# Keys and values of a cross-attention layer by Strassen's seven products, one level, sums kept in PSUM

## What is computed

```python
h_q = (rmsnorm(layernorm(x)) @ w_q.T).reshape(b, lq, H, DH)
h_k = (key_value_states @ w_k.T).reshape(b, lk, H, DH)
h_v = (key_value_states @ w_v.T).reshape(b, lk, H, DH)
score = jnp.einsum('bqhd,bkhd->bhqk', h_q, h_k) + position_bias[None]
score = softmax(where(m, score, -inf)); score = where(m, score, 0)
attn = jnp.einsum('bhqk,bkhd->bqhd', score, h_v).reshape(b, lq, H * DH)
x = x + layernorm(x) + attn @ w_out.T
W = NF4_CODE[w_codes] * absmax                      # decoded weights
x = x + layernorm(x) @ W.T + 2 * (layernorm(x) @ W_a @ W_b)
```

## Time and profile before

| | |
|---|---|
| median of 3 runs | 870.4 us (869.73 to 871.6) |
| profiled execution | 869.9 us, its span 868.1 us, mean granted clock of TensorE 0.998 |
| PE busy | 857.5 us (99%), 4292 matmuls |
| DVE, ACT, POOL busy | 513.0, 340.3, 366.2 us |
| DMA | 60.79 MB, mean 70 GB/s |

### The profile page before, as it was taken

The page is one execution under the profiler, slowest core; times in us unless marked ns, Lnnn a source line. Parts: engine busy times, 40 slices in busy tenths (PEclk is TensorE's granted clock), DMA queues, the critical chain, the costliest instruction groups (busy, mean ns, idle before and its releaser), DMA issues.

```text
span 868.1 us, 13682 instructions
## 1 busy us (share of the span) xinstructions
PE 857.5 (99%) x4292; PEld 723.9 (83%) x4292; DVE 513.0 (59%) x781; ACT 340.3 (39%) x939; POOL 366.2 (42%) x341
## 2 busy tenths in 40 slices
PE   9999999999999999999999999999999999999898
PEld 6887888888888888888888888888888888888786
DVE  5658682387615775176823867157751778328683
ACT  5346261253414444153622535135341436225332
POOL 0996272162704345043630627034450436408730
PEclk9999999999999999999999999999999999999999
DMA  8112331032310323013220323103230132202002
GB/s 314 52 42 83 105 102 52 0 107 71 102 34 23 112 68 107 4 50 114 80 71 0 104 74 97 39 19 112 59 112 12 47 104 61 78 0 65 25 13 86
DMA packets 52581, 60.79 MB, mean 70 GB/s; under 512 B 11312, under 2 KB 33456, under 8 KB 52432
## 3 DMA queue, kind: packets, MB, share of 16 engines
q1 hardware_dynamic: 52560, 60.54, 23.5%
HBM read 42.14 MB, written 2.10 MB: 51 GB/s over the span
## 4 chain that ended last, share of the span: by engine, by line
PE 82%; POOL 9%; DVE 3%; SPq 2%; issue 2%; DMA 1%; ACT 1%; POOLq 0%; DVEq 0%
PE proj_ps L815 49%; PE out_ps L815 21%; PE out_ps L922 6%; PE s_ps L862 5%; POOL scratch L379 2%; POOL scratch L402 2%; SPq L271 2%; POOL scratch L405 1%; POOL resid L382 1%; POOL bias L371 1%; DMA v<-ctx_dram 1%; DVE qk_lo L614 1%; DVE p L671 0%; DMA pT<-p_turned 0%; PE proj_ps L875 0%
## 5 line engine op out<-in xcount | busy, mean ns | idle before, releaser
L371 POOL TENSOR_TENSOR bias<-pos_raw,mask_add 128x1024 f32<-128x1024 f32 x32 | 69.0, 2155 | 396.5 <-DVE p L671 395.7
L709 DVE TENSOR_TENSOR resid<-out_ps,resid 128x512 f32<-128x512 f32 x136 | 92.2, 688 | 238.6 <-PE out_ps L815 238.6
L402 POOL TENSOR_SCALAR scratch<-codes 128x256 f32<-128x256 int32 x120 | 157.2, 1310 | 19.8 <-POOL scratch L405 16.3
L505 ACT ACTIVATE p_blocks<-p,neg_max 128x128 f32<-128x128 f32 x248 | 96.1, 389 | 136.0 <-DVE neg_max L673 136.0
L442 ACT ACTIVATE v<-proj_ps 128x512 f32<-128x512 f32 x64 | 38.3, 598 | 196.8 <-PE proj_ps L815 196.8
L614 DVE TENSOR_TENSOR qk_lo<-qk_raw,qk_hi 128x512 fp32r<-128x512 f32 x64 | 100.8, 1576 | 7.6 <-ACT qk_hi L442 7.6
L815 PE MATMUL proj_ps<-ctx_hi,qk_hi 128*128 128x512 f32 x256 | 103.2, 403 | 0.3 <-DVE ctx_lo L614 0.3
L815 PE MATMUL proj_ps<-xn_hi,qk_hi 128*128 128x512 f32 x256 | 102.5, 400 | 0.1
L815 PE MATMUL proj_ps<-wv_hi,ctx_hi 128*128 128x512 f32 x256 | 100.6, 393 | 0.0
L815 PE MATMUL proj_ps<-wv_lo,ctx_hi 128*128 128x512 f32 x256 | 100.2, 392 | 0.0
L815 PE MATMUL proj_ps<-ctx_hi,qk_lo 128*128 128x512 f32 x256 | 100.2, 391 | 0.0
(11 more groups left out here) (111 smaller groups left out, 1445.1 us busy)
## 6 DMA issues: line engine op xcount, KB each, us to landing
pT<-p_turned SPq DMA_DIRECT2D x496, 32.0 KB, 1.8
qk_raw<-k_dram SPq DMA_DIRECT2D x32, 256.0 KB, 2.8
qk_raw<-q_dram SPq DMA_DIRECT2D x32, 256.0 KB, 2.7
wo_raw<-wo_dram SPq DMA_DIRECT2D x32, 256.0 KB, 2.8
wv_raw<-wv_dram SPq DMA_DIRECT2D x30, 256.0 KB, 3.5
resid<-x_dram SPq DMA_DIRECT2D x2, 1024.0 KB, 10.7
pos_raw<-pos_dram SPq DMA_DIRECT2D x32, 64.0 KB, 2.9
out_dram<-resid SPq DMA_DIRECT2D x8, 256.0 KB, 2.1
```

The lines of the kernel that those rows point to most:

```text
L371: pool.tensor_tensor(bias[:, :, :], pos, mask_add[:, :, :], ALU.add).then_inc(bias_done, 1)
L402: then(pool.tensor_scalar(level if code == 0 else picked, codes[:, :], float(code), value, match, ALU.mult))
L505: e = act.activation(out(b), p[:, b, :].rearrange("p (k c) -> p k c", c=Q), ACT.Exp, bias=neg_max[:, b:b + 1], accum_out=prob_sum[:, b:b + 1])
L709: dve.tensor_tensor(resid[:, b, :], out_ps[bank][:, :], resid[:, b, :], ALU.add).then_inc(out_drained, 1)
```

## The change

Keys and values, `ctx @ w`, are each cut once in halves of the tokens, of the inputs and of the heads, and the eight block products are replaced by Strassen's seven. The halves of heads are the two heads of a pair for the keys, and two pairs of a group for the values. Weight and context are kept as sums and differences of blocks:

- The seven sums of the context are made once at the start (POOL `context_sum`, then hi and lo) and fill `ctx_hi` and `ctx_lo`, [P, 7, 2, 512].
- The sums of weights are made in place in `k_raw` and `wv_raw` on POOL (`weight_sum`): four subtractions of 128x256 for each of 16 pairs of heads, four of 128x512 for each of 8 groups. Each waits until DVE has split the block that it overwrites.
- `key_product`: 6 matmuls of 512 columns, seven times a pair, all in the odd head of the pair. `value_product`: 12 matmuls of 256 columns, 14 times a group.
- The products are added up in PSUM banks; ACT copies a bank where a result or a partial sum is wanted (four copies), DVE adds a bank to what was copied (three additions), for keys for each pair, for values in two halves of tokens (r) for each group.
- There is one `k_raw` of a whole pair (512 KB), and its load for the next pair waits for the last split of the pair before it. On SP it is issued at odd heads behind both `move_blocks`; before, one head's 256 KB was issued ahead of them.
- To make room, the buffers `bias`, `p_turned` and `w_ffn` are gone: the bias is written into `p`, so `make_bias` waits for `exp_done` in place of `biased`; blocks are turned in place, so the first `exps` of a head waits for `pT_loaded` of the head before; decoded slices go to DRAM and come back, the last through `last_ffn_loaded`. Eight PSUM banks are shared out anew, and `attend` writes the two banks of the scores, after `biased`.
- The residual's hidden part moves from POOL to ACT, and `x_stage` from DVE to ACT.

```diff
+PRODUCTS = 7
+BLOCK_A, BLOCK_B, BLOCK_C, BLOCK_D = range(4)
+WEIGHT_AT = (BLOCK_A, BLOCK_A, BLOCK_A, BLOCK_B, BLOCK_D, BLOCK_C, BLOCK_A)
+BANK_OF = (0, 1, 0, 0, 1, 2, 0)
+OPENS = (True, True, False, False, False, True, False)
+SUMS = 4
+SUMS_FOR = (0, 1, 3, 2, 0, 0, 4)
+RING = 4
+COPIES = 4
+ADDS = 3
...
-                        sp.wait_ge(k_lo_done, h + 2)
-                        load_k(h + 2)
+                    if not final:
+                        sp.wait_ge(p_turned_done, 2 * h + 1)
+                        sp.sem_inc(sp_passed, 1)
+                        sp.wait_ge(attn_done, 2 * h)
+                        move_blocks((0, 1))
+                        sp.wait_ge(p_turned_done, 2 * h + 2)
+                        move_blocks((2, 3))
+                    if j % 2 and not last:
+                        sp.wait_ge(k_lo_done, PRODUCTS * (m + 1))
+                        load_k(m + 1)
...
+            def weight_sum(n, raw, sums, count, step):
+                out, plus, minus = ((BLOCK_A, BLOCK_B, BLOCK_A), (BLOCK_B, BLOCK_D, BLOCK_B),
+                                    (BLOCK_A, BLOCK_D, BLOCK_A), (BLOCK_A, BLOCK_C, BLOCK_A))[n]
+                if n:
+                    passed(sums, SUMS * count + n)
+                if n != 1:
+                    passed(step, PRODUCTS * count + (1, 0, 2, 3)[n])
+                pool.tensor_tensor(raw[:, out, :], raw[:, plus, :], raw[:, minus, :],
+                                   ALU.subtract).then_inc(sums, 1)
...
+            def make_bias(slot):
+                pos = pos_raw[:, slot, :].rearrange("p (o k) -> p o k", o=1).broadcast_to([P, B, L])
+                pool.tensor_tensor(p[:, :, :], pos, mask_add[:, :, :], ALU.add).then_inc(bias_done, 1)
...
+                    if j == 1:
+                        key_sum(2, m)
+                        key_sum(3, m)
+                    if j == 2 and not last:
+                        for n in range(SUMS - 1):
+                            key_sum(n, m + 1)
+                    if j == G:
+                        value_sum(2, g + 1)
+                    if not (last and j == G - 1):
-                        passed(biased, 2 * h + 2)
+                        passed(exp_done, 2 * h + 2)
+                        passed(pos_loaded[(j + 1) % 2], 16 * (2 * g + (j + 1) // 2 + 1))
+                        make_bias((j + 1) % 2)
+                    if j == 2 and not last:
+                        key_sum(SUMS - 1, m + 1)
+                    for quarter in (((0, 1), (2, 3), ())[j - 1] if last else (j - 1,)):
+                        decode(g, quarter)
+                    if j == 3 and not last:
+                        passed(wv_loaded, 16 * (g + 2))
+                        value_sum(0, g + 1)
+                        value_sum(1, g + 1)
+                    if j == G:
+                        value_sum(3, g + 1)
+                        key_sum(0, m + 1)
...
+            def odd_head(g, j, last):
+                h = G * g + j
+                m = 2 * g + (j + 1) // 2
+                exps(h, 0, by_blocks)
+                if j == 1:
+                    split_k(m, 2, key_slot(j, 2))
+                copy_keys(m, 0)
+                if j == 1:
+                    split_k(m, 3, key_slot(j, 3))
+                copy_keys(m, 1)
+                exps(h, 1, by_blocks)
+                for hf in range(2):
+                    attention(h - 1, j - 1, hf, s_flat(hf))
+                for p_at in (4, 5):
+                    split_k(m, p_at, key_slot(j, p_at))
+                copy_keys(m, 2)
+                split_k(m, 6, key_slot(j, 6))
+                drain_q(h + 1, 0, query_bank(j, 0))
+                for i in range(2):
+                    split_wo(i, 2 * g + j // 2 + 1, wo_hi)
+                drain_q(h + 1, 1, query_bank(j, 1))
+                split_q(h + 2)
+                if j == 3:
+                    split_v(g + 1, 0)
+                copy_keys(m, 3)
...
+            def even_head(g, j, last):
+                h = G * g + j
+                m = 2 * g + (j + 1) // 2 + 1
+                if j == G:
+                    split_v(g + 1, 1)
+                elif not last:
+                    split_k(m, 0, key_slot(3, 0))
+                for hf in range(2):
+                    exps(h, hf, by_blocks)
+                if j == 2 and not last:
+                    split_k(m, 1, key_slot(3, 1))
+                drain_q(h + 1, 0, query_bank(j, 0))
+                for hf in range(2):
+                    attention(h - 1, j - 1, hf, s_flat(hf))
+                if j == 2 and not last:
+                    split_k(m, 2, key_slot(3, 2))
+                    split_k(m, 3, key_slot(3, 3))
+                drain_q(h + 1, 1, query_bank(j, 1))
+                if not last:
+                    split_q(h + 2)
...
+            for hf in range(2):
+                exps(H - 1, hf, in_place)
+            act.wait_ge(last_ffn_loaded, 16)
+            split_ffn(C - 1)
+            for hf in range(2):
+                act.wait_ge(turned, hf + 1)
+                copy(last_pT[:, hf * HB:(hf + 1) * HB, :], s_ps[hf][:, :, :]).then_inc(last_pT_done, 1)
...
+            def add_keys(m, n):
+                slot, hf, bank, p_at, copied = ((1, 1, 0, 3, 2), (1, 0, 1, 4, 3), (0, 0, 2, 5, 1))[n]
+                dve.wait_ge(keys_done, PRODUCTS * m + p_at + 1)
+                dve.wait_ge(keys_copied, COPIES * m + copied)
+                at = kT[:, slot, half(hf)]
+                dve.tensor_tensor(at, w_ps[bank][:, :], at, ALU.add).then_inc(keys_added, 1)
...
+                for hf in range(2):
+                    bias_and_max(h, hf)
+                if j == 1:
+                    for p_at in (2, 3):
+                        split_k(m, p_at, key_slot(j, p_at))
+                for hf in range(2):
+                    normalise(h, hf)
+                turn_blocks(h)
+                for hf in range(2):
+                    attention(h - 1, j - 1, hf, s_flat(hf))
+                for p_at in (4, 5, 6):
+                    split_k(m, p_at, key_slot(j, p_at))
+                add_keys(m, 0)
+                add_keys(m, 1)
+                for i in range(2):
+                    split_wo(i, h - 1 + i, wo_hi, wo_lo)
+                split_q(h + 2)
+                if j == 3:
+                    split_v(g + 1, 0)
+                add_keys(m, 2)
...
+                if j == G:
+                    split_v(g + 1, 1)
+                elif not last:
+                    split_k(m, 0, key_slot(3, 0))
+                for hf in range(2):
+                    bias_and_max(h, hf)
+                if j == 2 and not last:
+                    split_k(m, 1, key_slot(3, 1))
+                for hf in range(2):
+                    normalise(h, hf)
+                for hf in range(2):
+                    attention(h - 1, j - 1, hf, s_flat(hf))
+                turn_blocks(h)
+                if j == 2 and not last:
+                    for p_at in (2, 3):
+                        split_k(m, p_at, key_slot(3, p_at))
+                if last:
+                    for c in range(C - 1):
+                        split_ffn(c)
+                    return
+                split_q(h + 2)
+                for b in range(B):
+                    add_pair(o, b)
...
+            def key_product(m, p_at, slot, first=False):
+                hi, low = (first_hi, first_lo) if first else (ring_hi, ring_lo)
+                pe.wait_ge(k_lo_done, PRODUCTS * m + p_at + 1)
+                pairs = [((hi[:, slot, s * DH:(s + 1) * DH], low[:, slot, s * DH:(s + 1) * DH]),
+                          (ctx_hi[:, p_at, s, :], ctx_lo[:, p_at, s, :])) for s in range(2)]
+                three(w_ps[BANK_OF[p_at]][:, :], pairs, OPENS[p_at]).then_inc(keys_done, 1)
+            def value_product(g, p_at, r, banks):
+                if r == 0:
+                    pe.wait_ge(wv_lo_done, PRODUCTS * g + p_at + 1)
+                hi, low = (flat(t[:, 2 * value_region(p_at):2 * value_region(p_at) + 2, :])
+                           for t in (ring_hi, ring_lo))
+                bank = banks[BANK_OF[p_at]][r]
+                for i in range(2):
+                    at = slice((2 * r + i) * L, (2 * r + i + 1) * L)
+                    pairs = [((ctx_hi[:, p_at, s, at], ctx_lo[:, p_at, s, at]),
+                              (hi[:, s * 2 * DH:(s + 1) * 2 * DH], low[:, s * 2 * DH:(s + 1) * 2 * DH]))
+                             for s in range(2)]
+                    mm = three(bank[:, i * 2 * DH:(i + 1) * 2 * DH], pairs, OPENS[p_at] and i == 0)
+                mm.then_inc(values_done, 1)
...
+                pe.wait_ge(keys_added, ADDS * m)
+                pe.wait_ge(attn_lo_done, 2 * (h - 1) + 2)
+                scores(h, 0)
+                if j == 1:
+                    pe.wait_ge(values_copied, 2 * COPIES * (g + 1))
+                key_product(m, 0, key_slot(j, 0))
+                key_product(m, 1, key_slot(j, 1))
+                if j == 1:
+                    pe.wait_ge(values_added, 2 * ADDS * (g + 1))
```

(95 more changed lines are left out.)

1132 lines of the change are left out of this document (609 added, 523 removed).

## The result

| | before | after |
|---|---|---|
| median | 871.0 us (869.73 to 871.85, 4 runs) | 980.95 us (980.27 to 981.37, 4 runs) |
| ratio, 95% interval | | 1.1263 (1.1243 to 1.1282) |
| profiled execution's span | 868.1 us | 979.6 us |
| mean granted clock of TensorE | 0.998 | 0.953 |

The sign was right, the size was not: 941 us were forecast, with a range up to 962. The granted clock is a share of TensorE's full 2.4 GHz; at the lower of its two levels, 1.2 GHz, it is 0.5. From here on L numbers are lines of the changed kernel.

The account below looks back on a forecast made before the run. PE, busy 99% of the span and waiting for nobody, was taken as the bound. 868.1 - 34.6 (PE's work) + 84 (loop stalls) + 12 (start) + 10 (end) = 939.5 span, 941 us with 1.8 around it; range 852 to 962, likeliest case 920 to 962.

Parts of the forecast that it names:

- PE's work: Key and value products: 96 fewer key matmuls save 21.8 us, 256-column value matmuls at 0.120 save 12.8; 34.6 us less.
- stalls of the loop: PE's waits in the heads from late keys and the port: 12 us a group, 84 us over seven groups.
- start: Before head 1: late statistics of x delay norm and transpositions, head 1 at 70 to 75; 12 us of PE idle.
- end: Last attends: POOL's decode chain starts later and its slice is stored and loaded; PE idle 10 us.
- rival of weight loads not hidden: Value products: weight load not hidden behind 256 columns, 0.160 each; 54 us more, 995 us; chance 0.07.
- Late keys: Heads of j = 2: load_k behind the moves lands late, bias_and_max starts at 5.4, not 1.1; 2.1 stall at attend.
- case in between: Loop: late keys partly covered, 865 to 880 us; chance 0.09.
- The port: All heads: POOL's bias starts first and holds the port shared with DVE, so p_blocks waits about 2.1 us.
- rival that it does not matter: Port: DVE's p_blocks starts before POOL's bias, which then waits; late keys alone cost, 895 us; chance 0.22.
- milder reading: Odd heads: POOL's decoding does not block DVE, by the rows; blocking would cost some 20 us more.
- j by j: PE stalls in each head of a group: 2.0, 6.3, 1.6 and 2.1 us for j = 1 to 4.
- Nothing in the loop stalls: Rival: keys land in time, splits just in time, only start and end cost; 857 us; chance 0.16.

Follow-up runs that it names:

- e5: e3 with the next keys' and second value splits moved behind the softmax in even heads, POOL's sums behind its bias: 866.9 us, ratio 0.9952.
- e4: The changed kernel plus 168 unneeded matmuls on PE, ahead of the wait for attn_lo at the first output of even heads: 958.04 us, ratio 1.1009.
- e10: The changed kernel with e5's order of splits and sums and e2's later bias, keys still loaded behind all sixteen moves: 867.93 us, ratio 0.9964.
- e2: The changed kernel with POOL's bias waiting for p_done (after p_blocks) instead of exp_done: 930.35 us, ratio 1.0674.
- e3: The changed kernel with the next keys loaded between the two runs of eight moves, and with e2's later bias: 897.56 us, ratio 1.0307.
- e6: e3 with x's statistics moved earlier on DVE, ahead of later context and value splits at the start: 888.61 us, ratio 1.0199.
- e7: e3 without head 31's exps waiting for pT_loaded, and with the last slice's split behind last_pT's copies and attention: 887.28 us, ratio 1.018.

## Why the prediction was wrong in size

By its own terms, from the windows of before and after and the group of e5:

| term | forecast | measured |
|---|---|---|
| PE's work, seven groups and start | -34.6 | 7 x -4.4 = -31, and -4.3 in the start, not measured by itself |
| stalls of the loop | 84 | 84.4 + 31 - 32.0 (clock) = 83 |
| start | 12 | 18.4 + 4.3 - 8.6 (clock) = 14 |
| end | 10 | 8.7 - 3.0 (clock) = 6 |
| clock | none | 44, of which 38 under work |

- **The step that failed** is a term that is not there. "The clock was granted in full here" was read from the trace of before and carried into a kernel of which the same text says that PE will wait 12 us in each group. With 939.5 + 44 the sum is 983.5, against a span of 979.6. With the 38 us under work alone the likeliest case's 941 becomes 979, outside its range of 920 to 962. The column above takes the clock's loss off in full; what of it fell into idle time (3.0 in the start, 2.4 in the loop, 1.3 in the end) belongs to the stalls. e4 shows that the loss comes from PE's idling and is real time.
- **PE's work.** Right: 0.120 for 256 columns, 97.3 a group where 97 was worked out. The rival of weight loads not hidden (995) falls, close as its number came.
- **Late keys.** Right in place, and in size where nothing else had moved: bias_and_max 5.1 after the scores for 5.4. It is 3.2 to 3.7 behind the three heads of j = 1 in which the clock fell, and PE then does not wait at attend: the next head starts later against the load. The wait came in all seven groups, so the case in between (865 to 880) falls too. But e10 shows that the late landing costs only where the split stands ahead of bias_and_max: with the split moved, it costs nothing.
- **The port.** Right: p_blocks 2.60 for the forecast 2.7, and POOL won in 29 of 31 heads (22 times against a p_blocks, 7 times against a row_scale). The rival that it does not matter (895) falls, by 50.6 us in e2. The milder reading of the decoding's tensor_scalar held too, nearly: in e3 a ring_lo of 512 columns that began at 651.21 took 0.88 in place of 0.69 under a tensor_scalar from 650.94 to 652.22, which would have held it for 1.0 more if it blocked.
- **j by j**, the head's length less e5's: j = 1 2.3 or, with the clock falling, 3.9 (forecast 2.0), j = 2 7.8 to 8.1 with 1.7 of clock in four heads and 7.5 with 3.4 in the three where the clock was low for twice as long (6.3), j = 3 1.1 (1.6), j = 4 4.7 to 4.8 with 1.7 of clock in six heads and 1.3 in the first, where POOL's bias caught nothing and the clock did not fall (2.1). The last was too small by about 1 us in the six; which step of its working was short was not taken apart.
- **Nothing in the loop stalls** (857): not this kernel, but e10, which has start and end as in the change, shows it at 867.9; the clock's 17.3 us there (0.980 of 866.4) are more than the difference of 11.
- **Start.** The last statistics end at 47.3, not 43, and head 1 starts at 80.9, not at 70 to 75. e6 gets 8 of it back by moving the statistics of eight tiles forward, six of them into idle time of DVE. What it leaves, 59.5 for 49.4 before at head 0, was not taken apart.
- **End.** The 8.7 of the window look like the forecast's 10, but by luck: 3 of them are clock, and the place is another. PE's one long wait, 7.4, is for the softmax of head 31, whose exps on ACT wait 9.5 for the moves of head 30, though they write in place; the working took the exps' wait for moves as met in the loop and has none in the end. The slice did land late, as worked out (ACT waits 8.4 for it ahead of copies that do not need it), but PE had other work until then. e7 takes both waits away and gains 10.3 with POOL's chain as it was.

## What to carry to other kernels

Fewer matmuls pay only while PE waits for nobody: here the arithmetic was worth 35 us, and the waits around it with their clock cost over 140. When you sum waits that a change brings to a kernel with a full clock, add the matmuls that will run at 1.2 GHz behind them; here that was a third to nearly a half as much again. Before you make a late transfer earlier, look at what stands behind its consumer on the engines that work in order: the new order of splits and sums gained 75 us, and the early load, once order and bias were right, nothing.

## What was unexpected of the hardware

- **A short wait lowers the clock, but not each one.** 1.20 GHz came after 2.54 us of waiting at 505.93 and after 4.42 at 575.10, and lasted 3 to 4 us. The heads of j = 3, with a wait of 0.8 each, ran at 1.00 throughout (587.51 to 607.23 is one). Of the heads of j = 1 behind the first group, all with a wait of about 2 us for ring_lo, two of six have a fall (they take 22.5 us, the others 20.9). In e3 there is none in the loop: its waits there are 1.4 and 1.3 us at the longest, but for one of 2.0 in head 1.
- **The port blocks by kind of operand, not by size.** A row_scale of four columns, both inputs in SBUF, waited 1.7 us for POOL's bias. But an attn_lo with one input in PSUM, and the transposition with its one input, run untouched under it. In e3, DVE and then POOL in order of time:

```profile
621.19 1.28 DVE L842 TENSOR_TENSOR attn_lo<-s_ps,attn_hi 128x512 fp32r<-128x512 f32 x2
622.38 1.29 DVE L917 STREAM_TRANSPOSE p_blocks<-p_blocks 128x512 f32<-128x512 f32 x2
```

```profile
621.54 2.15 POOL L444 TENSOR_TENSOR p<-pos_raw,mask_add 128x1024 f32<-128x1024 f32 x1 [1.83 <-DVE p_blocks L910]
```

  Both DVE lines keep their usual length while the bias runs. So the bias behind p_done does not only shift the collision: what follows there is attention and turn. The Trainium skill, SBUF — State Buffer, section "SBUF: two separate sides", limits the shared port on DVE's side to operations with two SBUF inputs or in a two-port mode; with attn_lo and the transposition the trace agrees.
- **Idle PE can be cheaper busy.** 168 matmuls without use made the kernel 22.9 us faster (e4).
